# A selective scan with its loads of C issued ahead of those of B, and its D term as a diagonal matmul

## The reference

```python
x = x + 0.5 * ffn(layernorm(x))
x = x + mamba(layernorm(x))
x = x + 0.5 * ffn(layernorm(x))

def mamba(x):                                # N = 16 states, R = 128
    xz = einsum('btd,rd->btr', x, W_xproj)   # delta_r, B_mat, C_mat
    delta = softplus(einsum('btr,dr->btd', delta_r, W_dt) + b_dt)
    dA = exp(delta[..., None] * -exp(A_log))
    Bu = delta[..., None] * B_mat[:, :, None, :] * x[..., None]
    # h_t = dA_t * h_{t-1} + Bu_t ;  y_t = sum_n h_t[n] * C_t[n]
    return y + x * D_param

def ffn(x):                                  # 64 experts of rank 16, 4 chosen
    vecs = einsum('arh,bsh->bsar', A, x)
    routes = one_hot(top_k(norm(vecs), 4)).sum(-2) / 4
    v = einsum('bsa,bsar->bsr', routes, vecs)
    return x @ W.T + bias + einsum('bsa,ajr,bsr->bsj', routes, B, v)
```

## Time and profile before

| what | us |
|---|---|
| median of the runs of the kernel before | 2237.09 (2235.93 to 2238.24) |
| the profiled execution, its own time | 2232.72 |
| its span, slowest core (3) | 2231.2 |
| spans of the other cores | 2213.3 to 2229.8 |
| scan stage, core 3, from 589 to 1838 us | 1249 |
| VectorE busy in the whole span | 1360.9 (61%) |
| TensorE matmul busy in the whole span | 988.4 (44%) |

### The profile page before, as it was taken

One profiled execution on the slowest core, in us unless ns is written; L12 is line 12 of the kernel. 1 busy time (PEld: TensorE's weight loads), 2 busy tenths in 40 slices (PEclk: granted clock), 3 DMA queues, 4 the chain that ended last, 5 costly groups with the idle time before them and its releaser, 6 DMA issues.

```text
span 2231.2 us, 14425 instructions; the slowest of 8 cores (2213.3 to 2231.2 us)
## 1 busy us (share of the span) xinstructions
PE 988.4 (44%) x3834; PEld 333.7 (15%) x3834; DVE 1360.9 (61%) x1413; ACT 511.0 (23%) x517; POOL 172.9 (8%) x249
## 2 busy tenths in 40 slices
PE   3285899971322222222222222222222223758999
PEld 1042244430100000000000000000000000322443
DVE  2702411147588788887997987987887886223111
ACT  3012200030322322422323223223223213121000
POOL 0010011100000000000000000000000000010111
PEclk9597699985555555555555555555555556876999
DMA  8053075630121112112121121111212220341886
GB/s 200 0 49 37 2 70 57 60 34 0 65 85 42 60 67 75 52 43 85 42 67 61 42 85 42 64 64 42 85 43 63 75 30 0 38 47 23 114 114 100
DMA packets 159263, 129.75 MB, mean 58 GB/s; under 512 B 142304, under 2 KB 142560, under 8 KB 155088
## 3 DMA queue, kind: packets, MB, share of 16 engines
q0 software_dynamic: 151536, 110.33, 26.4%
q1 hardware_dynamic: 7648, 18.50, 2.6%
HBM read 155.09 MB, written 8.46 MB: 73 GB/s over the span
## 4 chain that ended last, share of the span: by engine, by line
DVE 49%; PE 25%; DMA 12%; issue 6%; ACT 5%; DVEq 1%; SPq 1%; POOL 0%; ACTq 0%; POOLq 0%
DVE U L696 24%; PE pb L532 10%; DVE U L691 8%; DMA xbr<-rowsD 8%; DVE U L711 7%; PE pb L536 5%; PE pb L373 4%; DVE xln L328 2%; DVE xln L331 2%; ACT mpool L657 1%; DMA ubufA<-Bf_T 1%; ACT mpool L654 1%; DVE mpool L461 1%; DVEq L62 1%; DMA x<-x_fm 1%
## 5 line engine op out<-in xcount | busy, mean ns | idle before, releaser
L717 PE MATMUL pb<-U,identS 128*128 128x512 bf16 x256 | 149.7, 585 | 924.0 <-DVE U L711 924.0
L696 DVE TENSOR_TENSOR_SCAN U<-U 128x1152 bf16<-128x1152 bf16 x171 | 437.5, 2558 | 17.7
L684 ACT ACTIVATE U<-mpool,acols 128x1152 bf16<-128x1152 f32 x171 | 214.7, 1256 | 490.7 <-DVE U L696 489.2
L544 DVE SCALAR_TENSOR_TENSOR x<-pb,x 128x512 f32<-128x512 f32 (+1 forms) x80 | 48.9, 611 | 346.2 <-PE pb L539 346.2
L696 DVE TENSOR_TENSOR_SCAN U<-wbufD,U 128x1152 bf16<-128x1152 bf16 x85 | 217.4, 2558 | 9.1 <-DVE U L691 0.5
L691 DVE TENSOR_TENSOR U<-U,vecs 128x1152 bf16<-128x1152 bf16 x256 | 194.1, 758 | 28.0 <-DVE U L711 1.8
L717 PEld LDWEIGHTS pb<-U,identS 128*128 128x128 bf16 x256 | 26.7, 104 | 1142.1 <-issue 1142.1
L684 ACT ACTIVATE wbufD<-mpool,acols 128x1152 bf16<-128x1152 f32 x85 | 106.7, 1256 | 244.9 <-DVE U L696 244.2
L720 PE MATMUL pb<-U,identS 128*128 128x512 bf16 x256 | 161.8, 632 | 0.0
L532 PE MATMUL pb<-xln,wbufC 128*128 128x512 bf16 (+1 forms) x640 | 128.8, 356 | 6.8 <-DVE U L505 4.7
L532 PE MATMUL pb<-xln,wbufD 128*128 128x512 bf16 (+1 forms) x640 | 124.5, 348 | 1.3 <-DMA ubufB<-Bf_T 0.8
(11 more groups left out here) (99 smaller groups left out, 1166.8 us busy)
## 6 DMA issues: line engine op xcount, KB each, us to landing
vecs<-rowsD POOLq DMA_DIRECT2D x32, 1152.0 KB, 6.9
xbr<-rowsD POOLq DMA_DIRECT2D x64, 288.0 KB, 7.4
sqr<-rowsD POOLq DMA_DIRECT2D x64, 288.0 KB, 7.0
x<-x_fm SPq DMA_DIRECT2D x8, 1152.0 KB, 18.4
wbufC<-W_T POOLq DMA_DIRECT2D x16, 512.0 KB, 8.6
wbufD<-W_T POOLq DMA_DIRECT2D x16, 512.0 KB, 8.9
out_fm<-x SPq DMA_DIRECT2D x16, 512.0 KB, 3.2
wbufA<-A_lhsT POOLq DMA_DIRECT2D x8, 512.0 KB, 7.5
```

Source lines behind the costliest of these rows:

```text
L544: e.scalar_tensor_tensor(xt(j, c0, n), bank[:, 0:n], 0.5, xt(j, c0, n), ALU.mult, ALU.add), sem="vres_" + tag)
L684: E.op("scalar", lambda e, k=k, ni=ni, dab=dab, pi=pi: e.activation(dab, deltaf[:, pi * TW:(pi + 1) * TW], AF.Exp, scale=acols[:, k * NST ...
L696: E.op("vector", lambda e, dab=dab: e.tensor_tensor_scan(U[:, _hh:_hh + TW], dab, U[:, _bu:_bu + TW], 0.0, ALU.mult, ALU.add), sem="vh")
L717: E.op("tensor", lambda e, woff=woff, ni=ni, b0=b0: e.matmul(b0[:, 0:512], ident[:], U[:, woff:woff + 512], start=(ni == 0), stop=False))
```

## The change

Two edits, both in the block loop of `_mamba`.

The loads: `cp_load(h + 2)` is now written ahead of `bq_load(g + 2)`, and the B load is written one state index later (`ni % 4 == 1`).

The D term: VectorE no longer scales 1024 columns of `xln` at the end of a block. At its start it scales the 128 x 128 identity by the tile's column of D, which gives a diagonal matrix, in a part of `mpool` that `deltaf` doesn't reach. The four last matmuls of a block take that diagonal as weights and `xln` as the moving operand. VectorE's wait for `tns` and TensorE's for the scaled columns go.

```diff
             banks = {0: (pb[4], pb[5]), 1: (pb[6], pb[7])}
+            for pi, k in enumerate(dts):
+                if dtb >= 1 and pi == 0:
+                    E.wait("vector", "tys", dtb * 2)
+                E.op("vector", lambda e, pi=pi, k=k: e.tensor_scalar_mul(
+                    mpool[:, 4608 + pi * 256:4608 + pi * 256 + P],
+                    ident[:], dcols[:, k:k + 1]), sem="vdg")
             if dtb >= 1:
                 E.wait("tensor", "vy", dtb * 2)
             for ni in range(NST):
...
-                if ni % 4 == 0 and g + 2 < 32:
-                    bq_load(g + 2)
                 if ni % 2 == 0 and h + 2 < 64:
                     cp_load(h + 2)
+                if ni % 4 == 1 and g + 2 < 32:
+                    bq_load(g + 2)
...
-                    if dtb >= 1 and ni == 0:
-                        E.wait("vector", "tys", dtb * 2)
...
-            E.wait("vector", "tns", (dtb * NST + NST - 1) * 2 + 2)
-            for pi, k in enumerate(dts):
-                woff = _ww0 if pi == 0 else _ww1
-                E.op("vector", lambda e, k=k, woff=woff: e.tensor_scalar_mul(
-                    U[:, woff:woff + TR], xlnt(k, WU, TR), dcols[:, k:k + 1]),
-                    sem="vwd")
-            E.wait("tensor", "vwd")
+            E.wait("tensor", "vdg", E.val("vdg"))
             for pi, k in enumerate(dts):
                 b0, b1 = banks[pi]
-                woff = _ww0 if pi == 0 else _ww1
-                E.op("tensor", lambda e, b0=b0, woff=woff: e.matmul(
-                    b0[:, 0:512], ident[:], U[:, woff:woff + 512], start=False, stop=True))
-                E.op("tensor", lambda e, b1=b1, woff=woff: e.matmul(
-                    b1[:, 0:512], ident[:], U[:, woff + 512:woff + 1024],
+                dg = mpool[:, 4608 + pi * 256:4608 + pi * 256 + P]
+                E.op("tensor", lambda e, b0=b0, dg=dg, k=k: e.matmul(
+                    b0[:, 0:512], dg, xlnt(k, WU, 512), start=False, stop=True))
+                E.op("tensor", lambda e, b1=b1, dg=dg, k=k: e.matmul(
+                    b1[:, 0:512], dg, xlnt(k, WU + 512, 512),
                     start=False, stop=True), sem="tys")
```

## The result

| | before | after |
|---|---|---|
| median of the runs, us | 2235.74 (10 runs) | 2193.54 (11 runs) |
| ratio | | 0.980, 95% interval 0.976 to 0.984 |
| scan, from the first L664 to the start of the last pair of adds, core 3 | 1259.1 | 1216.7 |
| the same, all cores | 1255.2 to 1260.1 | 1216.5 to 1216.7 |
| spans of the cores | 2213.3 to 2231.2 | 2166.5 to 2196.8 |

The kernel got 42.2 us faster by the medians, 1.9%, against a forecast of 2193 and a sum of 42.5 us. The interval of the ratio reaches to both sides of 0.98, so whether it is over 2% stays undecided, as the prediction had it. The interval reaches some 8 us to either side. Some executions fall into a slower state, in which the cores of one die show a lower granted clock; medians and ratios here are of the others alone.

What follows compares the result with a forecast made beforehand. VectorE was taken to bound the scan. C loads 35.8 plus D-term tail 12.6 minus diagonals 5.9 gave 42.5 us off 2232.7, so 2190.2, or 2194.6 by the median; forecast 2193 us, range 2184 to 2210.

Steps and rivals of the forecast that it cites:

- The bound and what counts: Selective scan: VectorE is the bound, busy 1069.6 of 1249 us; only shortening waits and work between blocks can help.
- the chain's 8% for xbr: Chain of waits: gives the xbr transfer 8% of the span, some 170 us, which isn't what the transfer costs.
- The C loads, 35.8 us: VectorE's 23 waits at L711 for xbr: 38.2 us less ordinary gaps, 35.8 us gained by loading ahead of B.
- POOL's issues at 0: Up to 62 C-load issues moved beside L691: cost VectorE 0; other bound 33 us.
- The tail, 8 x 1.58 = 12.6 us: Each block's end: without L726's scaling, L649 and L741 come 1.58 us earlier; 12.6 us gained over 8 blocks.
- the wait at the first add: Sign at the block boundary: VectorE's wait still near 2 us, but from a start 1.6 us sooner.
- The sum: Whole kernel: 35.8 + 12.6 - 5.9 = 42.5 us gained, ratio 0.981; scan stage shorter by 42 us.
- The diagonals, 5.9 us: VectorE between second L664 and first L691: two 128x128 diagonals, 0.73 us a pair with gaps, cost 5.9 us over 8.
- The clock: Last pass, TensorE bound: possible drop from 2.4 to 1.2 GHz; a granted clock below 0.9 would show it.
- the fourth rival: Last pass: half the stretch at TensorE's lower clock, +91 us, 2281 us; chance 0.04.

Runs made afterwards that it cites:

- experiment 1: Kernel before the change with only the order of the loads changed, C pair ahead of the B load: ratio 0.984, median 2204.9 us.
- experiment 3: Kernel before the change, code in its old order, with the C loads issued by SyncE's queue instead of POOL's: one run, 2208 us.
- Experiment 5: Changed kernel with each C load cut into two DMAs of 576 columns, 128 more POOL issues: one run, 2192 us.
- Experiment 4: Changed kernel with a block's two diagonals made ahead of its first L664, where VectorE waits for ScalarE: ratio 0.978, median 2195.8 us.
- experiment 2: Changed kernel with the loads put back into their old order, so the D term alone: ratio 0.9963, median 2233.1 us.
- experiment 7: Kernel of experiment 6 with L649 matmuls a step earlier and the next block's diagonals and both L664 ahead of the adds: ratio 0.959, median 2144.8 us.
- experiment 6: Kernel of experiment 4 with the next block's softplus begun during a block's last three steps: ratio 0.972, median 2171.5 us.

## Why the prediction was right

- *The bound and what counts.* VectorE, as the prediction had it. What went is not waits alone: the C loads' gain is. Of the tail's 12.6 us, 3.9 are waits (28.2 us at L726 and the adds before, 24.3 after), 7.8 are L726's own work, and the rest its gaps. VectorE's busy time in the scan of core 3 fell from 1076.5 to 1072.8 us, L726's 7.8 less the diagonals' 4.1. That the chain's 8% for xbr was not the price showed in experiment 1: the transfers are all still there and 35.7 us went.
- *The C loads, 35.8 us.* Measured 35.7. The cause was the queue's order (experiments 1 and 3). In the changed kernel no late load came in its place on any core; in the experiments there were one or two on some cores, of 0.2 to 1.9 us, and in experiment 3 one on each.
- *POOL's issues at 0.* Experiment 5, with twice as many.
- *The tail, 8 x 1.58 = 12.6 us.* L739 starts 3.04 us behind the last product instead of 4.61, so 1.57 each. L649 moved by the same, and L664 with it. One sign was given wrongly: the wait at the first add was to stay near 2 us and is 3.0. The prediction's own rows had it: the product ends at 887.78 and the add was to start at 890.81. The sum goes by the add's start and not by this wait, so it is not touched.
- *The diagonals, 5.9 us.* They take 0.255 us each; the line between the two nearest rows gave 0.257. That it came so close is in part luck, since the row of 64 columns does another operation than that of 1024. The pair takes 0.72 with its gaps, 5.8 in all. Experiment 4 shows that they were on the path.
- *The sum.* The scan of core 3 is 42.4 us shorter, forecast 42.5, and experiments 1 and 2 give the two parts, 35.7 and 6.8. This is what bears the account out. On the other cores the scan got 38.6 (core 0) to 43.4 us shorter, by what each had lost to xbr. That the medians agree to 0.3 us is luck: their interval reaches some 8 us either way, the slowest core isn't always the same, and the two profiled executions lie 34.4 us apart, mostly because the slowest core of the changed kernel took 13.5 us more behind the scan than core 3 had before.
- *The clock.* TensorE's granted clock in the last pass of the changed kernel was 0.97, the level of 2.4 GHz, as in the earlier trace rows; the fourth rival did not come (row of core 4):

```profile
1993.00:2196.00 203.00, 185.35 (x800) 76.82 (x800) 23.10 (x34) 0.42 (x1) 28.23 (x28) 0.97 0.73 96
```

What the prediction didn't have is a cheaper place for the diagonals, though the 1.55 us wait in front of L664 stood in its own rows.

## What to carry to other kernels

In a queue kept in order, write first the load whose condition is met first; a buffer that is free doesn't help behind a wait of a whole group. Read the price of a late transfer in the waits of the engine that needs it, take the ordinary gap off each, and not in the chain, which counts the transfer's whole flight. Then look at what an engine does behind a wait for another: work that doesn't depend on it (here the diagonals, the next block's L664) covers it. Experiments 4 and 7 took 5.5 and 24.4 us from the scan so, and moving ScalarE's softplus under the last steps (experiment 6) another 20.5; together more than the change itself.

## What the runs showed of the hardware that was not expected

The time of one C load went with what was issued beside it. The median from issue to landing, in the page's table of DMA issues, was 7.4 us for xbr before, right behind the 1152 KB of a B load:

```profile
xbr<-rowsD POOLq DMA_DIRECT2D x64, 288.0 KB, 7.4
sqr<-rowsD POOLq DMA_DIRECT2D x64, 288.0 KB, 7.0
```

It is 3.5 us in the changed kernel, where it goes alone:

```profile
vecs<-rowsD POOLq DMA_DIRECT2D x32, 1152.0 KB, 6.0
xbr<-rowsD POOLq DMA_DIRECT2D x64, 288.0 KB, 3.5
sqr<-rowsD POOLq DMA_DIRECT2D x64, 288.0 KB, 5.9
```

The sqr loads, of which the first still goes out behind the B load, take 5.9 us.

The changed kernel's scan repeats to 0.2 us over cores, while the stages behind it don't. From the start of the last pair of adds to the end the cores of the changed kernel took 383.6 to 405.5 us, those of before 388.3 to 396.1. The core with 405.5 is the slowest of the profile, and its TensorE waited for the weights of the last pass:

```profile
PE pb L532 <- DMA ubufA<-Bf_T: 11.0, 6, 3.2
...
PE pb L373 <- DMA wbufB<-A_lhsT: 4.7, 1, 4.7
PE pb L373 <- DMA wbufA<-A_lhsT: 2.6, 2, 1.3
...
PE pb L532 <- DMA ubufB<-Bf_T: 1.5, 3, 0.7
```

That is 19.8 us; on core 2, with 383.6 us, the same four sum to 4.1. So 15.7 of the 21.9 us between them are weights that came late, and this is wider than the D term's whole gain. The mean of the eight cores over these stages was 391 us before and 393 after, and 389 to 395 in the experiments: no sign that the change takes something back there, but it is the reason why the medians can't tell a quarter of a percent. Why one core's weights come late and another's don't stays open.
